# Attention 1's tail shared with four expert steps, the MLP begun in attention 0, and attention 1's small work in another order

## What is computed

```python
x = x + _layernorm(attn0(_layernorm(x)))   # 16 heads of 128, weights codes * scales
x = x + _layernorm(ffn0(_layernorm(x)))    # hidden 704, (silu(g) * u) @ down_w, each with scales
x = x + _layernorm(attn1(_layernorm(x)))   # 16 heads of 16, causal, w_attn (256, 768), w_proj
x = x + _layernorm(ffn1(_layernorm(x)))    # 16 experts of 128, the best 8 of each token; 2 shared
```

```python
routing_weights = jax.nn.sigmoid(h @ gate_w.T)
topk_w, topk_idx = jax.lax.top_k(routing_weights, K)          # K = 8
topk_w = topk_w / (jnp.sum(topk_w, axis=-1, keepdims=True) + 1e-06) * SCALE
eo = einsum('eti,eih->eth', silu(einsum('th,ehi->eti', h, Wg)) * einsum('th,ehi->eti', h, Wu), Wd)
out = silu(h @ sWg) * (h @ sWu) @ sWd + einsum('eth,te->th', eo, comb)
```

## Time and profile before

| | us |
|---|---|
| median of the runs | 2249.73 |
| the runs | 2250.08, 2246.76, 2249.73 |
| the profiled execution | 2251.21 |
| its span, first to last instruction | 2249.5 |
| TensorE busy | 2122.8 (94%) |
| VectorE busy | 1468.5 (65%) |
| ScalarE busy | 1186.2 (53%) |
| pool busy | 565.8 (25%) |
| mean granted clock of TensorE | 0.971 |

### The profile page before, as it was taken

How to read it: one execution, slowest core, us unless ns; L and a number is a source line. 1 busy time by engine, 2 the same in 40 slices (tenths; PEclk the granted TensorE clock), 3 DMA queues, 4 the chain that set the end, 5 groups by cost and what they waited for, 6 DMA issues and landing times. The chain is left out here.

```text
span 2249.5 us, 35911 instructions
## 1 busy us (share of the span) xinstructions
PE 2122.8 (94%) x12680; PEld 1710.5 (76%) x12680; DVE 1468.5 (65%) x2625; ACT 1186.2 (53%) x2159; POOL 565.8 (25%) x558
## 2 busy tenths in 40 slices
PE   6999999999999999999999998989889898899996
PEld 5888888888888888888888877764455445788885
DVE  6676676676676676676667775446766782655555
ACT  5565465465465465455556555526656764433333
POOL 3021031031031031021021005412333443544443
PEclk9999999999999999999999998988999997999998
DMA  2010010010010010010020002000000010110001
GB/s 81 1 41 2 1 41 2 1 41 2 1 40 2 1 41 2 1 41 2 1 41 29 1 10 73 1 8 4 4 4 6 1 36 15 36 36 22 22 1 38
DMA packets 37687, 41.03 MB, mean 18 GB/s; under 512 B 7936, under 2 KB 33408, under 8 KB 37504
## 3 DMA queue, kind: packets, MB, share of 16 engines
q1 hardware_dynamic: 37504, 38.57, 6.4%
HBM read 36.45 MB, written 2.10 MB: 17 GB/s over the span
## 5 line engine op out<-in xcount | busy, mean ns | idle before, releaser
L816 ACT ACTIVATE attn_probT_hi<-psum 128x512 fp32r<-128x512 f32 x512 | 278.4, 595 | 305.9 <-PE psum L678 305.9
L874 DVE TENSOR_REDUCE attn_neg_max<-psum 128x1 f32<-128x1024 f32 x256 | 313.1, 1223 | 193.0 <-PE psum L81 192.4
L931 DVE TENSOR_TENSOR attn_probT_lo<-psum,attn_probT_hi 128x512 fp32r<-128x512 f32 x512 | 327.2, 680 | 28.0 <-ACT attn_probT_hi L816 27.9
L790 ACT ACTIVATE attn_prob<-psum,attn_neg_max 128x1024 f32<-128x1024 f32 x256 | 286.7, 1120 | 6.5 <-DVE attn_neg_max L874 6.5
L678 PEld LDWEIGHTS psum<-ident_sb,attn_prob 128*128 128x128 f32 x2048 | 237.8, 141 | 61.9 <-DVE attn_probT_lo L931 13.3
L678 PE MATMUL psum<-ident_sb,attn_prob 128*128 128x128 f32 x2048 | 267.4, 274 | 11.2 <-ACT attn_prob L790 11.2
L607 POOL TENSOR_TENSOR attn_v_lo<-x_sb,attn_v_hi 128x512 fp32r<-128x512 f32 x64 | 82.0, 1281 | 762.1 <-ACT attn_v_hi L824 762.1
L81 PE MATMUL psum<-attn_probT_hi,attn_v_hi 128*128 128x512 f32 x512 | 212.3, 415 | 0.6 <-DVE attn_probT_lo L931 0.6
L2216 ACT ACTIVATE attn_probT<-psum 128x512 f32<-128x512 f32 (+3 forms) x384 | 163.9, 495 | 92.2 <-PE psum L2101 89.2
L81 PE MATMUL psum<-attn_key_hi,attn_q_lo 128*128 128x512 f32 x512 | 201.0, 393 | 9.8 <-issue 9.8
L81 PE MATMUL psum<-attn_key_hi,attn_q_hi 128*128 128x512 f32 x512 | 201.4, 393 | 4.9 <-DVE xT_lo L348 4.9
(11 more groups left out here) (222 smaller groups left out, 4855.0 us busy)
## 6 DMA issues: line engine op xcount, KB each, us to landing
attn_v_all<-in_moe_w SPq DMA_DIRECT2D x23, 384.0 KB, 3.0
acc_sb<-in_x SPq DMA_DIRECT2D x4, 512.0 KB, 6.0
x_sb<-in_wq_codes SPq DMA_DIRECT2D x8, 256.0 KB, 2.5
x_sb<-in_wq_scales SPq DMA_DIRECT2D x32, 64.0 KB, 3.0
x_sb<-in_wk_codes SPq DMA_DIRECT2D x8, 256.0 KB, 3.8
x_sb<-in_wk_scales SPq DMA_DIRECT2D x32, 64.0 KB, 4.5
x_sb<-in_wv_codes SPq DMA_DIRECT2D x8, 256.0 KB, 5.1
x_sb<-in_wv_scales SPq DMA_DIRECT2D x32, 64.0 KB, 5.6
```

What stands on the lines that cost most here:

```text
L790: nc.scalar.activation(prob[:, i % 2, :], scores(i).rearrange("p a b -> p (a b)"), ACT.Exp, bias=neg_max[:, i % 2:i % 2 + 1], accum_out=to ...
L816: nc.scalar.activation(probT[0][:, g % 2, half_tile * GT:(half_tile + 1) * GT, j * P:(j + 1) * P], ring(use).rearrange("p (t n) -> p t n", ...
L874: nc.vector.tensor_reduce(neg_max[:, i % 2:i % 2 + 1], scores(i), AX.XY, ALU.max, negate=True).then_inc(max_ready, 1)
L931: nc.vector.tensor_tensor(to[1], ring(use).rearrange("p (t n) -> p t n", n=P), f32(to[0]), ALU.subtract).then_inc(ring_free, 1)
```

## The change

**Attention 0 and the MLP.** The turns of norm groups 0 and 1 stand among the last half's last value products, in banks 2 to 5; ScalarE and VectorE take them there. The second part of the last output has a bank of its own, 1, and no longer waits for VectorE to add up what stood in the first. ScalarE has a one-column silu and the hi half of slice 0's weights ahead of the last o_hi, the pool its lo half; these halves lie in a part of xT that is written later, and the first step reads them there. VectorE scales slices 0 and 1 there. SyncE loads slice 1 in attention 0, and group 2 of x, which was loaded there, in the MLP; group 3 and attention 1's inputs wait until all six splits are done. The statistics and the normalising of group 2 move from attention 0's end into the MLP's start. The MLP's tables, and then attention 0's output and `begin_mlp` on TensorE, `begin_mlp` on ScalarE, `begin_norm` on VectorE and the MLP's SyncE:

```diff
-        X_ADD, X_STATS, X_ACT, X_TURN = {1: 2, 3: 3}, {2: 2, 5: 3}, {4: 2, 7: 3}, {1: 1, 6: 2, 10: 3}
+        X_ADD, X_STATS, X_ACT, X_TURN = {3: 2, 7: 3}, {4: 2, 8: 3}, {5: 2, 9: 3}, {7: 2, 11: 3}
+        SPLIT = {-1: 1, 0: 2, 1: 3, 2: 4, 3: 5, 4: 0}
-        slots = [("x", 0), ("step", 0)]
+        slots = [("step", 0)]
```

```diff
             def output(half, g, part, last=False):
                 ...
-                pe.wait_ge(out_done, use + 1)
+                if not (last and part):
+                    pe.wait_ge(out_done, use + 1)
+                bank = (out_bank, last_out_bank)[last and part]
...
+            def begin_mlp(part):
+                if part < after.ahead:
+                    after.turn(pe, part, last_turn_banks(part)).then_inc(after.turned, 1)
...
+            def begin_mlp():
+                nc.scalar.activation(neg_max[:, 0:1], neg_max[:, 0:1], ACT.Silu)
+                mlp.first_hi(act, first_scaled, first_hi)
+                for g in range(after.ahead):
+                    act.wait_ge(after.turned, g + 1)
+                    after.take_hi(act, g, last_turn_banks(g))
...
+                if i == tiles - 1:
+                    mlp.scale_first(dve, first_scaled)
...
             def _(sp):
-                for e in range(1, N):
+                for e in range(2, N):
                     sp.dma_start(staged[:, e - 1, :], self.w_dram[e]).then_inc(self.landed[min(e, 3)], 16)
+                sp.wait_ge(w_ready, 1)
+                before.load_x(sp, before.groups - 2)
                 sp.wait_ge(row_kept, 1)
-                sp.wait_ge(w_ready, 1)
+                sp.wait_ge(w_ready, N)
                 before.load_x(sp, before.groups - 1)
                 early.sync(sp)
```

```diff
-        1: [("shift", 0, 1, 0), ("sums", -1, 1, 0)],
-        2: [("spread", -1, 1, 0), ("stack", 1, 1, 0), ("stack", 1, 1, 1)],
-        3: [("stack", 1, 1, 2), ("stack", 1, 1, 3)],
+        0: [("stack", 1, 1, 0), ("stack", 1, 1, 1)],
+        1: [("shift", 0, 1, 0), ("sums", -1, 1, 0), ("stack", 1, 1, 2), ("stack", 1, 1, 3)],
+        2: [("spread", -1, 1, 0)],
+        3: [("project", 2, 0, 0)],
...
-        7: [("project", 2, 0, 0)],
...
-    LAST_Y, LAST_OUT = 1, 4
+    LAST_Y, LAST_OUT = (TOTAL + 1, TOTAL + 2), 4
...
-    LOAD_IN, SPLIT_AT, BEGIN_AT = HALVES - 1, (TOTAL - 12, TOTAL - 7), TOTAL - 10
+    SPLIT_AT = (TOTAL - 12, TOTAL - 9, TOTAL - 4, TOTAL)
+    GATE_AT = {TOTAL - 10 + 2 * p: p for p in range(moe.EARLY + 1)}
+    DOWN_AT = {TOTAL - 7 + 2 * p: p for p in range(moe.EARLY)}
+    END = TOTAL + len(moe.steps) - moe.EARLY + 2
```

```diff
-    FIRST_EXPERTS = 5
+    FIRST_EXPERTS = 7
+    EARLY = 4
...
+    def early_down(self, pe, p, part, bank):
+        v = self.steps[p][2]
+        if part == 0:
+            pe.wait_ge(self.lo_done, p + 1)
+        for j in range(2):
+            at = slice((2 * part + j) * P, (2 * part + j + 1) * P)
+            mm = three_passes(self.nc, bank[:, j * C:(j + 1) * C], [h[p % 2][:, at] for h in self.hid],
+                              [self.half_of(half, v, slice(self.cols_down, self.cols)) for half in range(2)])
+        return mm
...
     def gate_up(self, pe, p):
-        if p >= 2:
+        if 1 <= p <= self.EARLY:
+            pe.wait_ge(self.prod_done, p)
+        elif p > self.EARLY:
             pe.wait_ge(self.prod_done, p - 1)
...
+        if g in DOWN_AT:
+            found += [("down", DOWN_AT[g], 0, part) for part in range(2)]
...
-                if g == BEGIN_AT:
-                    pe.wait_ge(max_free, HALVES * HALF_FILLS)
-                    moe.gate_up(pe, 0)
+                if g in GATE_AT:
+                    if GATE_AT[g] == 0:
+                        pe.wait_ge(max_free, HALVES * HALF_FILLS)
+                    moe.gate_up(pe, GATE_AT[g])
...
-                if g == TOTAL - 2:
-                    act.wait_ge(weighed, (HALVES - 1) * QUADS)
-                    moe.silu(act, 0)
+                if g in GATE_AT:
+                    if GATE_AT[g] == 0:
+                        act.wait_ge(weighed, (HALVES - 1) * QUADS)
+                    moe.silu(act, GATE_AT[g])
```

291 lines of the change are left out of this document (168 added, 123 removed).

## The result

| kernel | median, us | lowest to highest | runs |
|---|---|---|---|
| before | 2250.08 | 2243.06 to 2258.96 | 11 |
| after | 2234.13 | 2226.12 to 2244.34 | 11 |

The ratio is 0.9932, with a 95% interval of 0.9914 to 0.995: 15.3 us faster (11 to 19), and inside the range of 2212 to 2240. The forecast was 2224, though, so 11 of the 26.5 us did not come. The profiled execution of the kernel after took 2234.03 us, its span is 2232.3.

A forecast was written before the change was run, and what follows sets the result against it. It took TensorE's work at full clock, its waits and its 1.2 GHz losses as the bound. 8.6 + 3 + 14.9 = 26.5 us off the profiled 2251.2 gave 2224 us (2216 to 2232; 8 in 10: 2212 to 2240).

The forecast's parts named there:

- part 1: Attention 0 to MLP: fewer waits at the border, less half clock, turns out of the MLP; 8.6 us gained (4 to 10).
- part 3: Four expert steps moved from the end into attention 1's tail, filling waits and slow clock; 14.9 us gained (4 to 20).
- part 2: Attention 1's halves: new order of stacks and projection, 0.5 us gained in each of six halves; 3 us.
- the tail is 27.9 + 16.7 + 6.0 + 2.5 = 53.1 us, 8.4 us more: Attention 1's tail: full-clock work, four added steps, waits and clock loss, in that order; 53.1 us against 44.7.
- 6.6 us of waits and clock: Behind the attention: 3.0 us of half clock, 1.9 of the hidden_lo wait, 1.7 of half clock after it gone.
- make_y now cut in two, 1.9 gone: Behind the attention: hidden_lo stands behind make_y on the pool; cutting make_y removes 1.9 of the 3.39 us wait.
- (a): Tail: table loads make TensorE wait for ScalarE's whole chain at each early gate, 13 us more; 2237 us, chance 0.20.
- (b): Tail keeps full clock with only the old waits, and the halves gain 6 us; 2213 us, chance 0.15.
- (c): Attention 1's new order costs one 3.4 us wait in each of seven halves, 24 us; 2251 us, chance 0.07.
- (d): Slower: the tail stays at 1.2 GHz throughout, its 44.6 us of work costing 44.6 more; 2266 us, chance 0.05.
- the 1898 given: Sign: the first expert step behind the attention should start near 1898, where it was 1901.67.
- 4.17 us each: Sign: the 67 expert steps behind the attention should take 4.17 us each, without a wait of over 2 us.

The follow-up runs named there:

- e1: The kernel before with part 1 of the change alone, attention 1 and experts as before; ratio 0.9981 to before.
- e2: e1 plus attention 1's new order of small work (stacks, projection, weight split earlier), old tail and experts; 2235.55 us, ratio 0.992 to before.
- e6: e2 with FIRST_EXPERTS = 7 in place of 5; 2231.6 us, ratio 0.9917 to before.
- e5: e2 with norm group 1's pieces five quads earlier (76 to 80), its normalising and turns earlier too; 2232.41 us, ratio 0.9918 to before.
- e9: e5 with FIRST_EXPERTS = 7: the change without early steps and cut make_y; 2226.76 us, ratio 0.9911 to before.
- e3: The kernel after with a copy replacing the four early steps' silu, so without their table loads; 2228.46 us, ratio 0.9897 to before.
- e11: The kernel after with eight first experts, make_y in one piece, and early silu by tanh without table loads; 2220.53 us, ratio 0.9879 to before.
- e12: e11 with make_y in two pieces, the last output (quad 101), norm group 3, group 2's turn and router one step later; 2223.13 us, ratio 0.9894.
- e7: The kernel after with the last make_y in one piece again; 2229.09 us, ratio 0.9908 to before.
- e8: The kernel after with FIRST_EXPERTS = 8 in place of 7; 2228.56 us, ratio 0.99 to before.
- e4: The kernel after, unchanged, run and traced again; 2234.86 us, ratio 0.9928 to before.

## Why the prediction was right, and where it was off

The time lies in the range, and part 1's mechanism held. Otherwise it was partly luck: the largest term, part 3's 14.9 of 26.5 us, gave nothing, and the result came within the range because part 2 gave more than its 3 us.

**Part 1, forecast 8.6.** The mechanism held: 5.3 us at the border for 5.6, the first products at the full clock (2.4 us rather than 1.2). Mis-sized was what I gave for the MLP: 3.0 us, of which 1.2 came, since a wait of 2.66 us on the pool is new. Sum 6.5 by trace; 4.3 (0 to 9) by time.

**Part 2, forecast 3.** Too small. I had bounded it by one wait of 0.66 us a half; in seven halves 6 to 8 us of waits went (30.6 and 31.8 us before and in e1, 24.0 and 24.4 in e2 and e6), and no slow clock. Which of the moved jobs did it is not shown. By the times it is 13.7 us, give or take 8, and it carries, with part 1, the whole of the result (e2).

**Part 3, forecast 14.9.** This is where the missing time is; by the traces it is a loss of 6.6 us against e2, by the times it is level with e2. The runs take it apart: the norm's pieces gain 2.3 us (435.8 to 433.4, e5), seven first experts 3.5 (to 429.9, e9), and the early steps with the cut make_y cost 12.5 (to 442.4). Three terms failed.

First, "the tail is 27.9 + 16.7 + 6.0 + 2.5 = 53.1 us, 8.4 us more": from the first early gate the stretch grew by 11.2. Its waits are 4.5 us, so the 6.0 was near. But I had let the 10.6 us of slow clock fall to 2.5 because dense products stood there, and 5.4 were lost. e5 shows what lowers it: with the norm's pieces out of the tail 14.7 us lost became 5.4, without an early step. With the pieces gone, the four steps add 18.6 to 19.7 us for 16.7 taken away, and the 5.4 lost stay 5.4 to 6.1. They fill neither waits nor slow clock. Without the table loads (e3, e11, e12) they add 14.9 to 15.6.

Second, the pieces of the norm had to go five quads earlier for chunk 1 to be ready at quad 88. I had that in part 2's bounds only; it is up to 1.8 us in half 6 and 4.5 ahead of the early gate (e5), more than made up by the 8.4 in the tail.

Third, behind the attention I expected 16.7 us of work to leave and 6.6 us of waits and clock to be regained, and the stretch shrank by 10.9. The first gate products are indeed at the full clock, but the waits on the pool grew from 3.39 to 5.5 us, and more slow clock than went came back at 1952: over the whole stretch 9.0 us were lost to it before and 12.8 are after. "make_y now cut in two, 1.9 gone" was wrong in sign as the change stands (e7), since the wait for y_lo was left out of the sum.

**The table loads**, 3 us by e3 and 3.7 by e11. The row's 1.28 us for one gave the right size. The Trainium skill, ScalarE: Activation LUTs, section What ACT_TABLE_LOAD costs, has 2.66 us a switch, which would make an estimated 11 us more of waiting. The traces exclude that much, and no drain shows behind a load here: the next activation starts 0.01 us after it. The Trainium skill, same page, section Table sets: the hidden batching unit, lists tanh beside exp in one set. The runs agree (7 table loads with tanh, where silu had 15), and e11's stretch is what that is worth.

**The rivals.** (a) is refuted by e3. (b) fell with the tail, which kept its slow clock and took 11.2 us more, though the halves gained what it gave them; (c) fell with the halves, which became shorter. (d) did not happen: the stretch with the early steps had a clock of 0.90.

**The signs.** The first gate product behind the attention came at 1895.42, near the 1898 given. "4.17 us each" for the 67 steps behind it was a misreading: 4.17 is a step in the middle of the experts, and with waits, turns and splits between them the steps behind the attention took 4.7 us each before already (335.4 us for 71) and take 4.8. Two waits of over 2 us stand there, 3.12 and 3.28 us, besides those of 3.2 and 3.3 near the end that before has too.

## What to carry to other kernels

Work moved into a stretch with low clock need not raise that clock by being dense: here it lost 5.4 us with the four steps and 5.4 without. Ask first what makes the stretch thin, and try to take that away alone. A step that is moved pulls along whatever has to be ready for it, and those pieces have a cost and a gain of their own, here 6.3 us where they went and 8.4 us where they had been. When a wait's bracket names an engine, look at which of the candidates ended last to the hundredth, and at what the waiting instruction needs: here it was VectorE's xT_lo and not the pool's weights, and a change of one number removed the wait.

## What was unexpected of the hardware

The clock's losses can repeat exactly: from half 1 to the end, two traces of the kernel after agree within 0.2 us in every stretch, slow clock and all. Two traces are not a rule, though. Kernels whose code is the same up to there fall into a few values: half 1 takes 45.8 or 48.3 us in the traces with the new order, half 2 takes 47.6 or 50.1, half 6 of the kernels with early steps 44.3, 45.4, 46.1 or 46.7, and the runs of the kernel after range over 18 us. Half 0 took between 38.9 and 45.6 us in traces with the new order, with a granted clock of 1.00 or down to some 0.8, and the start of attention 1 18.5 or 22.3 us. In attention 0 the last value product's start differed by 4.7 us. So a difference of 2 to 3 us between two single traces says little unless it is a wait, or comes back in a third trace. What sets the dip at 1952 in the kernel after stays open: it follows the wait for chunk 3, is shorter without that wait (e8), and e3, which has the wait, lost 1.7 us in the 23 us behind it where e4 lost 8.1.
